# Decoder layer on one core: folded keys copied out of the banks by ScalarE alone, with the order of calls laid anew

## The chip, the cores and the metric

The kernel runs on one core of a Trainium2 chip. A core has five engines that each work through their own list of instructions in order and meet only through semaphores: TensorE (PE, matmuls, with its weight loads PEld), VectorE (DVE), ScalarE (ACT), GpSimd (POOL) and SyncE (SP), which here only issues DMAs. The metric is the device time of one execution in microseconds, lower is better. Before the change it is 623.12 us, the median of three runs (623.07 to 624.21).

## The reference

One decoder layer on 8 elements of 256 tokens with 256 channels, all fp32:

```python
x = x + attn(layernorm(x), W_q, W_k, W_v, W_o)      # 16 heads of 16, rotary, causal
x = x + xattn(layernorm(x), ctx, ctx, mask,         # 16 heads of 64 over 77 context rows
              W_Q, W_K, W_V, W_O)
x = x + ffn(layernorm(x))                           # 256 -> 1024 -> 256, exact gelu

# in ffn both linears are
Wq = fake_quant_weight(W)                           # 8 bits, one scale for the tensor
base = jnp.einsum('bsi,oi->bso', x, Wq) + b
lora = jnp.einsum('bsr,or->bso', jnp.einsum('bsi,ri->bsr', x, A), B)
return base + SCALING * lora
```

The part that the change touches is the cross-attention's keys. `softmax((x W_Q)(ctx W_K)^T / 8)` is computed as `x (W_Q (ctx W_K)^T)`: the query weight is folded into the keys once, at the start, for all elements. The folded keys are a matrix of 256 rows and 16 heads x 616 context rows.

## The kernel before, in words

Every fp32 product is made of three matmuls, because each operand is held as a hi piece and a lo piece: hi x hi, hi x lo, lo x hi (`product`, L732 to L734). So a result of TensorE that is used again is first copied out of its bank as the hi piece by ScalarE (`copy`, L1409), and then VectorE or GpSimd takes the difference as the lo piece (`low`, L1846; GpSimd L548, L555, L569).

The work is software-pipelined over the 8 elements. Each engine runs `first()`, then five times `step(a, b, n, m)`, then `drain()`; in a step element a is in its causal attention, b in its cross-attention and feed-forward, n in its projections, m in its first norm. Each engine's `first`, `step` and `drain` is a list of calls written out by hand; nothing else sets the order. Between engines only the semaphore waits in the called functions hold.

`first()` covers 0 to about 218.6 us: loads and splits of all weights, the folded keys, the values of the context (`values2`), the projections of elements 0 to 3, the causal attention of 0 to 2, and cross-attention and feed-forward of element 0. The calls that matter here:

- `keys(m)`, m = 0 to 7: TensorE makes the keys of two heads (12 matmuls of 128x308); ScalarE copies the hi piece `kT` out (0.68 us), VectorE the lo piece.
- `fold(m, k)`, k = 0, 1: TensorE multiplies them with the query weight (L777, `wo_hi`/`wo_lo` in the trace, since that memory holds the query weight first), in two halves. The bank pairs 3/4 and 5/6 are used in turn, so a half waits until the half two places before is copied out. The copy goes to one of three places in SBUF (`fold_slots`: two in `ck_raw`, one in `work`), from which SP's `store_folded` sends it to DRAM (L351); a place is free again when its store has landed (`fold_st`).
- Of the 32 halves, ScalarE copies the 16 with k = 0 and VectorE the 16 with k = 1 (L1819).
- `scores(a, g, ..)` (L883) makes scores in three banks by turns, and VectorE's `maxima(a, h)` (L1893, two per g) finds the row maxima; `scores` of g waits for the maxima two heads before. After `transpose_max`, ScalarE's `maxima(a)` and SP's `shifts(a)`, `shifted(a, g)` (L904) makes the scores again, less their maxima, and ScalarE takes the exponential (`exponentials`, L1442). For elements 0 to 2 `shifted` has one pair of banks, so each waits for the exponential before it.
- `rotary` (VectorE, L1877), `rotate` (GpSimd, L563, L564, L569) and `rotated` (ScalarE) make the rotated q and k; SP stores them (`store_rotated`) and loads them back in stacked form (`stacks`).
- `statistics_b`, `inverse_deviation` (GpSimd, L574) and `norm_b` (VectorE, L1841) make the norm ahead of the cross-attention (`norm_b(b, 0)`) and the feed-forward (`norm_b(b, 1)`).
- `quantise` (VectorE, L1760 to L1766) rounds `wpj_raw` and `wfc_raw`, three passes each; GpSimd's `split_lo` (L548) makes the lo pieces of the context, WV, WO, WO2 and the projection weight.

Of the kernel before, what the change touches and what calls it, by code (L numbers as in the profile page):

```python
# [38 lines left out]
def decoder_layer(nc, x, ctxT, mask, wqT, wkT, wvT, woT, wQT, wK, wV, wO, wfcT, bfc, Afc, BfcT,  # L39
# [25 lines left out]
    with ExitStack() as ctx:  # L65
# [251 lines left out]
        def _(sp):  # L317
# [116 lines left out]
            def first():  # L434
                first_input()
                weight(QKV_W)
                weight(CTX_W)
                weight(WK_W)
                lora_columns()
                trig_tables()  # L440
                load_x(1)
                weight(WQ_W)
                weight(PJ_W)
                store_rotated(0)
                weight(WV_W)
                load_x(2)
                stacks(0, 0)
                residual_input(0)
                store_folded(0, 0)
                weight(WO_W)  # L450
                store_folded(0, 1)
                stacks(0, 1)
                store_folded(1, 0)
                store_folded(1, 1)
                store_folded(2, 0)
                store_folded(2, 1)
                store_rotated(1)
                store_folded(3, 0)
                shifts(0)
                store_folded(3, 1)  # L460
                store_folded(4, 0)
                store_folded(4, 1)
                store_folded(5, 0)
                load_x(3)
                store_folded(5, 1)
                store_folded(6, 0)
                stacks(1, 0)
                store_folded(6, 1)
                store_folded(7, 0)
                store_folded(7, 1)  # L470
                stacks(1, 1)
                weight(WO2_W)
# [3 lines left out]
                weight(FC_W)  # L476
                biases()
                context_values(0)
                store_rotated(2)
                stacks(2, 0)  # L480
                load_x(4)
                stacks(2, 1)
                context(1)
                residual_input(2)
                store_rotated(3)
                shifts(2)
                stacks(3, 0)
                stacks(3, 1)
                context_values(1)
# [25 lines left out]
        def _(pool):  # L515
# [90 lines left out]
            def first():  # L606
                inverse_deviation(rs_a, lna_ve, lna_rs, 0)
                split_lo(CTX_W)
                rotate(0, 0)
                inverse_deviation(rs_a, lna_ve, lna_rs, 1)  # L610
                rotate(0, 1)
                rotate(1, 0)
                rotate(1, 1)
                lora_rows()
                inverse_deviation(rs_a, lna_ve, lna_rs, 2)
# [4 lines left out]
                split_lo(WV_W)  # L620
                causal(0, 4)
                causal(0, 5)
                causal(0, 6)
                causal(0, 7)
                split_lo(WO_W)
# [103 lines left out]
        def _(pe):  # L729
# [1597 lines left out]
```

## Time and profile before

| | us |
|---|---|
| median of 3 runs | 623.12 |
| the profiled execution | 619.42 |
| its span (first to last instruction) | 617.7 |
| TensorE busy | 498.4 (81%) |
| VectorE busy | 389.0 (63%) |
| ScalarE busy | 291.4 (47%) |
| GpSimd busy | 252.5 (41%) |
| granted TensorE clock, mean | 0.953 of full speed |

TensorE has the largest share of busy time and 60% of the chain that ended last. The shares are means over stages of very different make. In the first 218.6 us the kernel prepares everything that is shared by all elements, and TensorE stands still more often; from there the five steps follow each other at about 63 us (the last two are shorter, 60 us), and then the drain of 88.8 us. A wait counts where it stands on TensorE in a stage in which nothing else is ahead of it; idle time of the other engines costs nothing by itself. A granted clock under 1 in a stage means that for part of it TensorE ran at 1.2 instead of 2.4 GHz.

### The profile page before, as it was taken

The page shows a single profiled execution, that of the slowest core. Times are in us where ns is not written, and L with a number is a line of the kernel's source. Part 1 is how long each engine was busy: PE and PEld are TensorE (multiplying, and loading weights), DVE is VectorE, ACT ScalarE, POOL GpSimd, SP SyncE. Part 2 cuts the span into 40 slices and gives each one's busy share as a digit, 9 for nine tenths or more (in the row PEclk, how much of TensorE's full clock was granted, in tenths as well). Part 3 has the DMA queues.
Part 4 walks back from the last instruction along what each step waited for, and adds up shares of the span by engine and source line. Part 5 has one row for each costly group of instructions (what it writes and reads, how often), then busy time and mean ns, then how long its engine had stood idle before and what let it go on. Part 6 is the DMA issues. An engine that isn't in the chain of part 4 may idle for free.

```text
span 617.7 us, 11686 instructions
## 1 busy us (share of the span) xinstructions
PE 498.4 (81%) x4320; PEld 416.9 (67%) x4320; DVE 389.0 (63%) x1079; ACT 291.4 (47%) x464; POOL 252.5 (41%) x351
## 2 busy tenths in 40 slices
PE   3577889599857879798879887988797879688986
PEld 3566667366646667587758865886586758677876
DVE  5669533877785089448945795479536943767532
ACT  4324454335455425482548344833583448343724
POOL 5551162537163633346234632464245134525310
PEclk9798999889977999899989998999999989899999
DMA  8696479355220414061406140714070210300000
GB/s 299 203 259 253 184 238 267 119 198 133 59 85 4 109 67 136 25 120 52 135 14 131 52 136 2 142 51 118 5 140 19 83 40 2 101 2 21 1 19 17
DMA packets 57496, 62.40 MB, mean 101 GB/s; under 512 B 6832, under 2 KB 52544, under 8 KB 57440
## 3 DMA queue, kind: packets, MB, share of 16 engines
q1 hardware_dynamic: 55936, 56.71, 33.1%
q0 software_dynamic: 1504, 4.95, 2.2%
q8 instruction: 34, 0.56, 0.4%
q14 instruction: 22, 0.18, 0.1%
HBM read 38.28 MB, written 23.10 MB: 99 GB/s over the span
## 4 chain that ended last, share of the span: by engine, by line
PE 60%; DVE 19%; ACT 6%; issue 6%; POOL 2%; DVEq 0%; POOLq 0%; ACTq 0%
PE banks L732 11%; PE banks L733 10%; PE banks L734 10%; PE banks L996 6%; PE banks L1054 5%; DVE banks L1893 3%; PE banks L1007 3%; PE banks L883 2%; DVE c_lo L1846 2%; PE banks L979 2%; PE banks L904 2%; ACT probs L1442 2%; DVE work L1841 1%; DVE mx L1956 1%; DVE work L1962 1%
## 5 line engine op out<-in xcount | busy, mean ns | idle before, releaser
L1893 DVE CUSTOM_DVE_ANT_0 banks<-banks,causal_qk 128x256 f32<-128x256 f32 (+1 forms) x256 | 83.7, 388 | 12.1 <-PE banks L883 7.6
L589 POOL TENSOR_SCALAR_AFFINE_SELECT probs<-probs 128x256 f32<-128x256 f32 x128 | 49.5, 414 | 100.0 <-ACT probs L1442 99.6
L578 POOL TENSOR_TENSOR work<-work,rc 128x616 f32<-128x616 f32 x32 | 39.9, 1247 | 105.0 <-DVE rc L1970 105.0
L1442 ACT ACTIVATE probs<-banks 128x768 f32<-128x768 f32 x64 | 50.8, 811 | 31.3 <-PE banks L904 27.4
L1409 ACT ACTIVATE work<-banks 128x1024 f32<-128x1024 f32 (+1 forms) x34 | 32.6, 962 | 34.2 <-PE banks L996 33.9
L555 POOL TENSOR_TENSOR ck_lo<-ck_raw,ck_hi 128x308 fp32r<-128x308 f32 x56 | 47.9, 881 | 0.0
L1846 DVE TENSOR_TENSOR c_lo<-banks,c_hi 128x512 fp32r<-128x512 f32 x32 | 22.0, 688 | 40.1 <-ACT c_hi L1409 40.1
L883 PE MATMUL banks<-k_stack,q_stack 62*128 62x256 f32 (+1 forms) x256 | 28.9, 304 | 22.2 <-DVE mneg L1893 22.2
L996 PE MATMUL banks<-ident,work 128*128 128x128 f32 (+1 forms) x256 | 36.9, 291 | 10.3 <-DVE c_lo L1846 9.5
L732 PE MATMUL banks<-wo_hi,c_hi 128*128 128x256 f32 x128 | 39.8, 311 | 6.1 <-DVE c_lo L1846 5.6
L1409 ACT ACTIVATE c_hi<-banks 128x512 fp32r<-128x512 f32 x32 | 19.2, 599 | 52.3 <-PE banks L1007 44.2
L883 PEld LDWEIGHTS banks<-k_stack,q_stack 62*128 62x128 f32 x256 | 20.0, 191 | 34.7 <-DVE mneg L1893 21.1
L1474 ACT ACTIVATE work<-work 128x616 f32<-128x616 f32 x32 | 22.9, 716 | 41.1 <-DVE work L1962 41.1
L996 PEld LDWEIGHTS banks<-ident,work 128*128 128x128 f32 (+1 forms) x256 | 30.1, 150 | 15.4 <-issue 13.7
L904 PE MATMUL banks<-q_stack,k_stack 64*128 64x128 f32 (+1 forms) x256 | 30.4, 322 | 9.9 <-ACT probs L1442 8.9
L732 PE MATMUL banks<-ck_hi,xbT_hi 128*128 128x308 f32 x112 | 37.9, 339 | 0.0
L732 PE MATMUL banks<-wpj_hi,hid_hi 128*128 128x256 f32 x128 | 37.9, 296 | 0.0
L733 PE MATMUL banks<-wo_lo,c_hi 128*128 128x256 f32 x128 | 37.1, 290 | 0.0
L734 PE MATMUL banks<-wo_hi,c_lo 128*128 128x256 f32 x128 | 36.8, 288 | 0.0
L733 PE MATMUL banks<-wpj_lo,hid_hi 128*128 128x256 f32 x128 | 36.5, 285 | 0.0
L734 PE MATMUL banks<-wpj_hi,hid_lo 128*128 128x256 f32 x128 | 36.4, 285 | 0.0
L1893 DVE DVE_READ_ACCUMULATOR2_ANT mneg<- 128x1 f32 x256 | 36.1, 141 | 0.0
(223 smaller groups left out, 1595.0 us busy)
## 6 DMA issues: line engine op xcount, KB each, us to landing
ck_raw<-ck_dram SPq DMA_DIRECT2D x28, 308.0 KB, 4.5
ck_dram<-ck_raw SPq DMA_DIRECT2D x11, 616.0 KB, 3.5
rot_dram<-rot_s_hi SPq DMA_DIRECT2D x16, 256.0 KB, 2.1
rot_dram<-rot_s_lo SPq DMA_DIRECT2D x16, 256.0 KB, 2.1
q_stack<-rot_dram SPq DMA_DIRECT2D x32, 128.0 KB, 3.5
k_stack<-rot_dram SPq DMA_DIRECT2D x32, 128.0 KB, 3.3
ck_dram<-work SPq DMA_DIRECT2D x5, 616.0 KB, 4.1
v<-v_dram SPq DMA_DIRECT2D x8, 308.0 KB
```

What stands on the lines that cost most here:

```text
L555: last = pool.tensor_tensor(ck_low(b, k, g), raw, ck_high(b, k, g).bitcast(F32), ALU.subtract)
L578: pool.tensor_tensor(sc2[g % 2], sc2[g % 2], rc2[:, g % 2].rearrange("p q a -> p q a ()").broadcast_to([P, QT, 4, S2]), ALU.mult).then_inc ...
L589: last = pool.affine_select(out=diagonal, in_=diagonal, compare_op=ALU.is_ge, fill=0.0, base=0, pattern=[[0, 2], [1, P]], channel_multipli ...
L732: pe.matmul(dst, w[0], x_[0], start=first, stop=False, **kw)
L733: pe.matmul(dst, w[0], x_[1], start=False, stop=False, **kw)
L734: return pe.matmul(dst, w[1], x_[0], start=False, stop=last, **kw)
L883: mm = pe.matmul(halves(banks[p])[:, 1 - q, 0:keys_q], q_stack[rows, g, q * P:(q + 1) * P], k_stack[rows, g, 0:keys_q], start=(q == 1), st ...
L904: mm = pe.matmul(halves(bk + p)[:, 1 - k, k * P:T], k_stack[rows, g, k * P:(k + 1) * P], q_stack[rows, g, k * P:T], start=(k == 1), stop=( ...
L996: mm = pe.transpose(bank[0:width, 5 + c, p * T + q * P:p * T + (q + 1) * P], sc2[g % 2].rearrange("p q a s -> p (q a s)")[:, at:at + width ...
L1409: act.activation(dst, src, ACT.Copy).then_inc(done, 1)
L1442: act.activation(probs[:, n:n + 2, :], bank[:, bk:bk + 2, P:4 * P], ACT.Exp, scale=SCALE).then_inc(p_ok, 1)
L1893: last = dve.tensor_tensor_reduce(out=scores_q, in0=scores_q, in1=causal_qk[:, 1 - q:2].rearrange("p a n -> p (a n)"), scale=-1.0, scalar= ...
```

## The change

VectorE's `fold` is removed, and ScalarE's `fold` gets k as a parameter and copies all 32 halves. The same banks, places and semaphores are used; VectorE keeps `keys`, the lo pieces. Beside this the lists of calls in `first()` are written in another order on all five engines, and two calls change places in `step()`.

```diff
-            def fold(m, half):
-                i = KD * m
-                act.wait_ge(fold_ps, 4 * m + half + 1)
+            def fold(m, k, half):
+                i = KD * m + k
+                act.wait_ge(fold_ps, 2 * i + half + 1)
                 if half == 0 and i >= FS:
                     act.wait_ge(fold_st[i % FS], 16 * (i // FS))
-                at = 3 + 2 * ((5 * m + 1 + half) % 2)
-                copy(folded(i, half), bank[:, at:at + 2, 0:HS].rearrange("p a (b s) -> p b a s", s=S2), fold_ok[0])
+                at = 3 + 2 * ((5 * m + 3 * k + 1 + half) % 2)
+                copy(folded(i, half), bank[:, at:at + 2, 0:HS].rearrange("p a (b s) -> p b a s", s=S2), fold_ok[k])
...
-            def fold(m, half):                       # VectorE
-                i = KD * m + 1
-                dve.wait_ge(fold_ps, 4 * m + half + 3)
...
-                dve.tensor_copy(folded(i, half), bank[:, at:at + 2, 0:HS].rearrange("p a (b s) -> p b a s", s=S2)) \
-                    .then_inc(fold_ok[1], 1)
```

On SP the loads at the start, and on TensorE the calls up to the first scores, read:

```diff
 first_input()                      # SP
+weight(WK_W)
+weight(CTX_W)
+load_x(1)
 weight(QKV_W)
-weight(CTX_W)
-weight(WK_W)
-lora_columns()
 trig_tables()
-load_x(1)
 weight(WQ_W)
...
 project(0, 0)                      # TensorE
+keys(0)
 project(0, 1)
-project_v(0)
-keys(0)
 fold(0, 0)
 keys(1)
+fold(0, 1)
+fold(1, 0)
+project_v(0)
+keys(2)
 transpose_a(1)
-fold(0, 1)
+fold(1, 1)
 project(1, 0)
+fold(2, 0)
+keys(3)
 project(1, 1)
-fold(1, 0)
-keys(2)
 scores(0, 0, 2)
```

Further on, TensorE's `lora_down(0)` and `lora_down(1)` move from between the shifted scores of element 0 to behind `transpose_a(2)` and `scores(1,0)`; `output_a(0)` and `project(2,0)` move ahead of `values2(1)`, and `values2(2)` behind `scores(1,0)`; and the four `hidden(0, g)`, which stood behind `scores(2,4)`, `scores(2,7)` and `transpose_max(2)`, stand behind `scores(2,2)`, `scores(2,3)`, `scores(2,5)` and `transpose_max(2)`. On SP `context(1)` moves ahead of `store_rotated(2)`. In `step()` ScalarE's `hidden(b,3)` goes ahead of `context_keys(b+1,3)` and VectorE's `context_lo(b,0)` ahead of `maxima(a,6)`.

ScalarE's list from the keys of m = 5 to the last exponentials of element 0, before (`ck_raw` and `work` are the fold copies, `kT` the keys, `probs` the exponentials):

```order
L1409 ACTIVATE kT<-banks 128x616
L1442 ACTIVATE probs<-banks 128x768
L1409 ACTIVATE ck_raw<-banks 128x616 x2
L1409 ACTIVATE kT<-banks 128x616
L1442 ACTIVATE probs<-banks 128x768 x2
L1409 ACTIVATE ck_raw<-banks 128x616
L1442 ACTIVATE probs<-banks 128x768
L1409 ACTIVATE ck_raw<-banks 128x616
L1442 ACTIVATE probs<-banks 128x768 x2
L1409 ACTIVATE kT<-banks 128x616
```

and now, from the keys of m = 6:

```order
L1409 ACTIVATE kT<-banks 128x616
L1380 ACTIVATE wo_hi<-wo_raw 128x512
L1409 ACTIVATE work<-banks 128x616
L1442 ACTIVATE probs<-banks 128x768
L1409 ACTIVATE work<-banks 128x616
L1442 ACTIVATE probs<-banks 128x768
L1409 ACTIVATE ck_raw<-banks 128x616
L1442 ACTIVATE probs<-banks 128x768 x2
L1409 ACTIVATE ck_raw<-banks 128x616
L1409 ACTIVATE kT<-banks 128x616
L1442 ACTIVATE probs<-banks 128x768 x2
L1409 ACTIVATE rot<-banks 128x512
```

The first exponential stood behind the keys of m = 5 and stands behind those of m = 6 and the first half of the last fold of m = 5, with the copies of both k among the exponentials.

GpSimd's list from the rotation of element 2 (`rot`) over the stores of the context's values (`v_dram`) to the keys of element 0, before:

```order
L569 TENSOR_TENSOR rot_s_lo<-rot,rot_s_hi 128x512
L544 DMA v_dram<-work 128x1024 x4
L544 DMA v_dram<-v 104x1024
L574 TENSOR_TENSOR rs_b<-rs_b,half_a 128x2
L555 TENSOR_TENSOR ck_lo<-ck_raw,ck_hi 128x308 x2
```

and now:

```order
L569 TENSOR_TENSOR rot_s_lo<-rot,rot_s_hi 128x512
L544 DMA v_dram<-work 128x1024 x3
L548 TENSOR_TENSOR wo_lo<-wo_raw,wo_hi 128x2048
L544 DMA v_dram<-work 128x1024
L574 TENSOR_TENSOR rs_b<-rs_b,half_a 128x2
L544 DMA v_dram<-v 104x1024
L555 TENSOR_TENSOR ck_lo<-ck_raw,ck_hi 128x308 x2
```

The lo split of the output weight WO2 (`wo_lo` 128x2048) now stands between these stores; it stood behind the last `affine_select` of element 1.

GpSimd's list around the second deviation of element 0 (`rs_b`, from `statistics_b(0,1)`), before:

```order
L574 TENSOR_TENSOR rs_b<-rs_b,half_a 128x2
L563 TENSOR_TENSOR rot<-probs 128x256
L564 TENSOR_TENSOR rot<-probs 128x256
L569 TENSOR_TENSOR rot_s_lo<-rot,rot_s_hi 128x512
L548 TENSOR_TENSOR wpj_lo<-wpj_raw,wpj_hi 128x2048
L574 TENSOR_TENSOR rs_a<-rs_a,half_a 128x2
```

and now:

```order
L574 TENSOR_TENSOR rs_b<-rs_b,half_a 128x2
L548 TENSOR_TENSOR wpj_lo<-wpj_raw,wpj_hi 128x2048
L574 TENSOR_TENSOR rs_a<-rs_a,half_a 128x2
L563 TENSOR_TENSOR rot<-probs 128x256
L564 TENSOR_TENSOR rot<-probs 128x256
L569 TENSOR_TENSOR rot_s_lo<-rot,rot_s_hi 128x512
```

The lo split of the feed-forward's second weight moved from behind the rotation of element 3 to right behind that deviation.

## Rows read from the trace of the kernel before

**Rows 1.** Busy time by stage: start:end, length, five engines with counts, PEclk, DMA share, GB/s.

```profile
0.00:24.80 24.80, 8.99 (x52) 8.13 (x53) 16.67 (x25) 10.63 (x10) 16.64 (x23) 0.97 0.74 249
24.80:89.80 65.00, 52.08 (x444) 42.22 (x444) 38.45 (x109) 26.60 (x39) 22.74 (x33) 0.90 0.74 236
89.80:128.30 38.50, 29.13 (x169) 22.93 (x168) 24.81 (x99) 14.06 (x26) 14.28 (x19) 0.88 0.62 180
128.30:150.80 22.50, 21.50 (x215) 16.27 (x215) 17.23 (x25) 12.32 (x17) 12.66 (x21) 0.98 0.62 183
150.80:169.80 19.00, 15.94 (x142) 13.55 (x140) 15.43 (x20) 6.22 (x11) 6.70 (x5) 1.00 0.33 86
169.80:194.00 24.20, 15.97 (x103) 13.68 (x100) 19.59 (x89) 12.74 (x23) 10.86 (x9) 0.79 0.17 56
218.60:528.90 310.30, 263.84 (x2428) 221.25 (x2427) 204.24 (x620) 158.13 (x259) 128.35 (x190) 0.98 0.29 72
```

**Rows 2.** Groups of instructions, 24 to 92 us: count, busy us, mean ns, idle before.

```profile
L1409 ACT ACTIVATE ck_raw<-banks 128x616 f32<-128x616 f32 x10 | 6.8, 684 | 12.2 <-PE banks L777 12.2
L1442 ACT ACTIVATE probs<-banks 128x768 f32<-128x768 f32 x8 | 6.5, 812 | 4.1 <-PE banks L904 4.0
...
L1819 DVE COPY ck_raw<-banks 128x616 f32<-128x616 f32 x12 | 9.3, 792 | 3.0 <-PE banks L777 3.0
...
L1846 DVE TENSOR_TENSOR kT<-banks,kT 128x616 fp32r<-128x616 f32 x8 | 6.4, 798 | 16.7 <-ACT kT L1409 16.7
```

**Rows 3.** TensorE's waits, 24.8 to 89.8 us: total us, times, longest.

```profile
PE banks L777 <- DVE kT L1846: 6.9, 4, 4.4
PE banks L883 <- DVE mneg L1893: 4.5, 3, 2.4
PE banks L777 <- ACT ck_raw L1409: 1.9, 2, 1.2
PE banks L732 <- ACT work L1409: 1.5, 2, 1.3
PE banks L904 <- ACT probs L1442: 0.9, 1, 0.9
PE banks L777 <- DVE ck_raw L1819: 0.8, 2, 0.7
PE banks L777 <- DVE work L1819: 0.4, 1, 0.4
```

**Rows 4.** Timeline, ScalarE then TensorE: start, length, instruction, idle before and releaser.

```profile
11.36 1.91 ACT L1380 ACTIVATE hid_hi<-hid_raw 128x2048 fp32r<-128x2048 f32 x1 [0.82 <-DMA hid_raw<-in_wK]
...
24.81 0.88 PE L777 MATMUL banks<-kT,wo_hi 64*128 64x308 f32 x4 [4.36 <-DVE kT L1846]
...
31.52 0.56 PE L777 MATMUL banks<-kT,wo_hi 64*128 64x308 f32 x4 [0.75 <-ACT ck_raw L1409]
```

**Rows 5.** TensorE, 89.8 to 128.3 us: a wait, then `values2(3)` and what follows.

```profile
PE banks L883 <- DVE mneg L1893: 5.1, 5, 1.1
...
107.74 0.50 PE L732 MATMUL banks<-wfc_hi,ck_hi 128*128 128x512 f32 x1
...
110.73 0.45 PE L883 MATMUL banks<-k_stack,q_stack 62*128 62x256 f32 x4
```

**Rows 6.** Line 1760's durations (ns, min/median/max, first and last start); GpSimd's timeline.

```profile
L1760 DVE TENSOR_SCALAR wpj_raw<-wpj_raw,winv x1: 1285/1285/1285, 57.4 to 57.4; 128x2048 f32<-128x2048 f32 x1
L1760 DVE TENSOR_SCALAR wfc_raw<-wfc_raw,winv x1: 4975/4975/4975, 148.8 to 148.8; 128x2048 f32<-128x2048 f32 x1
...
148.14 4.58 POOL L548 TENSOR_TENSOR wo_lo<-wo_raw,wo_hi 128x2048 fp32r<-128x2048 f32 x1
```

**Rows 7.** 169.8 to 194 us: TensorE's longest wait; `norm_b(0,1)` and GpSimd beside it.

```profile
PE banks L883 <- DVE mneg L1893: 5.8, 5, 2.5
...
176.54 1.46 DVE L1841 TENSOR_SCALAR work<-x,mv_b,rs_b 128x256 f32<-128x256 f32 x2 [0.16 <-POOL rs_b L574]
...
177.08 0.77 POOL L564 TENSOR_TENSOR rot<-probs 128x256 f32<-128x256 f32 x1
```

More of the change, by code:

```diff
@@ L1160, in first @@
                 shifted(1, 0)
-                lora_down(3)
                 shifted(1, 1)
@@ L1528, in first @@
[L1528 to L1545 removed]
+                fold(0, 1, 0)
@@ new lines, in first @@
+                fold(0, 1, 1)
+                fold(1, 0, 0)
+                fold(1, 0, 1)
+                split_hi(WV_W)
+                keys(2)
+                xaT_part(1)
+                values(0)
+                fold(1, 1, 0)
+                fold(1, 1, 1)
+                fold(2, 0, 0)
+                keys(3)
+                fold(2, 0, 1)
+                rotated(1, 0)
+                fold(2, 1, 0)
+                fold(2, 1, 1)
+                fold(3, 0, 0)
+                fold(3, 0, 1)
@@ L1546, in first @@
+                keys(4)
+                fold(3, 1, 0)
+                fold(3, 1, 1)
+                fold(4, 0, 0)
+                fold(4, 0, 1)
+                maxima(0)
+                keys(5)
+                rotated(1, 1)
+                fold(4, 1, 0)
+                fold(4, 1, 1)
+                fold(5, 0, 0)
+                fold(5, 0, 1)
+                keys(6)
+                split_hi(WO_W)
+                fold(5, 1, 0)
                 exponentials(0, 0, 2)
-                fold(5, 0)
@@ L1991, in first @@
             def first():
+                clear_queries()
                 statistics_a(0)
-                clear_queries()
                 norm_a(0)
+                split_lo(WK_W)
+                xaT_part(0)
                 split_lo(QKV_W)
-                xaT_part(0)
+                statistics_a(1)
                 rotary(0, 0)
-                statistics_a(1)
-                split_lo(WK_W)
-                rotary(0, 1)
-                norm_a(1)
                 split_lo(WQ_W)
                 keys(0)
+                rotary(0, 1)
+                keys(1)
+                norm_a(1)
                 largest(1, PJ_W)
-                keys(1)
+                keys(2)
                 xaT_part(1)
-                fold(0, 0)
                 rotary(1, 0)
-                fold(0, 1)
+                statistics_a(2)
+                keys(3)
                 rotary(1, 1)
-                keys(2)
+                largest_of_all(1)
+                norm_a(2)
                 maxima(0, 0)
@@ L2084, in first @@
                 norm_b(0, 0)
+                clear_values()
+                norm_a(3)
                 xbT_part(0, 0)
-                clear_values()
                 add_lora(1, PJ_W, 2)
                 softmax2(0, 0)
+                softmax2(0, 1)
+                sums2(0, 0)
                 add_lora(1, PJ_W, 3)
-                sums2(0, 0)
-                softmax2(0, 1)
-                norm_a(3)
+                statistics_a(4)
                 largest(0, FC_W)
```

350 lines of the change are left out of this document (158 added, 192 removed).

## The prediction

> **What bounds the kernel now.** I read the stages first, then TensorE's waits inside them, then the instructions behind the waits. In the table of stages [rows 1] the reader is to see TensorE's busy time against each stage's length: 263.84 of 310.30 us in the five periodic steps, but 9.0 of 24.8, 52.1 of 65.0, 29.1 of 38.5, 15.9 of 19.0 and 16.0 of 24.2 us in parts of the start-up (0 to 218.6 us), at a granted clock of 0.90, 0.88 and 0.79 in three of them. No other engine is full there: in the fold stage VectorE has 38.5 of 65 us, ScalarE 26.6. TensorE works through an in-order list and waits for hand-overs. The steps keep their order but for two calls: `context_keys(b+1,3)` goes behind `hidden(b,3)`, and `context_lo(b,0)` ahead of one `maxima`. TensorE's waits in a step stand at other places (scores on `mneg`, `c_lo` of later groups), so I cost both at nothing; if that cover fails, 0.3 us a step, 1.5 in all, either way. What can be won or lost lies in the start-up, where TensorE is idle for about 55 us in all.
>
> **The copies themselves.** VectorE loses 16 copies of 0.79 us, 12.7 us in all; ScalarE gains 16 of 0.68, 10.9 us [rows 2]. Its load in the fold stage goes from 26.6 to 37.5 of 65 us. TensorE's waits for VectorE's copies were 0.8 + 0.4 = 1.2 us [rows 3], so the move alone is worth 1.2 at most; VectorE's free time counts only where VectorE was late with something else. That a copy on ScalarE ends 0.1 us sooner is worth nothing: the ring of two bank pairs hides it behind the next fold's matmuls, and would give 16 x 0.1 without them.
>
> **Term 1, up to the first fold (24.8 us before).** TensorE's last wait here was 4.36 us, for `kT` [rows 4]. Now the keys' weight and the context are loaded first, and the 0.79 MB of q, k and v weights stand behind x[1], which waits for the first norm (about 6.8 us). The bytes up to and with them are 3.0 MB; before, 2.7 MB had landed when ScalarE could split `hid_raw` at 11.36 us [rows 4]. So they land near 11.9; their hi and lo splits cost 1.5 and 1.8 us in the timeline, and `project(0,0)` starts at 15.2 instead of 10.4. It takes 2.6 us (twelve matmuls at 1.2 GHz, as before), `keys(0)` 1.75 and `project(0,1)` 1.4: 21.0. The lo pieces of the folded query weight and of the keys are ready about 22.3. The first fold so starts 2.5 us before its old 24.81, but `project_v(0)` (1.4 to 1.7) is still owed: +1.0. Bounds: the weights land 2 us later, -1.0; everything 1 us sooner with the earlier norm, +2.0.
>
> **Term 2, the fold stage, 24.8 to 89.8.** Item by item, walking TensorE's new list by hand with the old durations:
> - VectorE's copies are no longer waited for: +1.2 [rows 3].
> - `kT` (hi on ScalarE, then lo on VectorE, 0.68 + 0.80 [rows 2]) left 2.5 us of waits after the first one (6.9 less 4.36), in three places. Now only `keys(1)` and `keys(6)` have nothing but a first half of a fold between them and the half that needs their bank: 1.7. +0.8.
> - The first fold and `keys(1)` ran at 1.2 GHz after the 4.36 us gap: four matmuls in 0.88 us that take 0.56 later [rows 4]. Both together took 5.2 us where 3.1 do. The gap is now about 1.3 us: +2.1.
> - `scores(0,0)` stands right behind `project(1,1)` and waits until `rotary(1,1)` has read it, two VectorE instructions of 0.69: -1.4.
> - Score waits were 4.5 [rows 3]. Now `largest_of_all` and `norm_a(2)` stand on VectorE ahead of the first `maxima`, and two passes of the quantisation (1.3 and 1.2 us) among the others; I find waits of 1.9, 1.0, 1.7, 0.5 and 0.4, together 5.5. -1.0.
> - Waits for ScalarE were 1.9 + 1.5 + 0.9 = 4.3 [rows 3]. The eight exponentials of 0.81 [rows 2] have fewer of TensorE's folds between them than before (two and one `keys`, where five and two `keys` stood), so I find five waits of 0.4 to 1.1 (3.2 in all) and 0.8 where two folds now follow each other. +0.3.
> Sum +2.0. Bounds: of 12.9 us idle at most 5 can go, as the chains above stay; at worst ScalarE, serving folds and exponentials in one line, adds five waits of its 0.68, and the sum is -1.4.
>
> **Term 3, 89.8 to 128.3.** `values2(2)` (107.74 to 110.73 for its like, 3.0 us [rows 5]) no longer stands ahead of `scores(1,0)`, one `lora_down` (1.0) does: 2.0 sooner. VectorE sets this stage: TensorE waits 5.1 us for its maxima. VectorE takes in two `add_lora` and `up_weights` and gives `statistics_a(3)` away, +0.9 us of work. +1.0. What hides the rest: the v stores on GpSimd's queue slip behind a split of 4.58 us, which still ends before `clear_values` wants them; without that cover, -1. SP's `lora_columns` moves behind `shifts(0)`, 20 us ahead of its reader. Bounds -1 to +2. The stage after it has TensorE busy 21.5 of 22.5 us [rows 1]: nothing.
>
> **Term 4, the quantisation of `wfc`.** Its first step took 4.975 us, the same form on `wpj_raw` 1.285 [rows 6]. GpSimd's `wo_lo` split ran from 148.14 to 152.72; VectorE's instruction ends 1.1 us after it, near its own undisturbed length: it stood still meanwhile. Behind it stand `attention(1)` and `c_lo`, for which TensorE then waited. The split moves some 40 us ahead, beside maxima. VectorE wins up to 3.7 us; TensorE's idle time in the stage is 3.06 [rows 1], and some 0.5 of that stays for the c pieces: +2.5, bounds 0 and 3.0. SP now holds `context(1)` ahead of `store_rotated(2)`, to about 144 us instead of 130; its reader is at 165 or later, so that is hidden.
>
> **Term 5, scores of element 2, 169.8 to 194.** The four `hidden` now go between the scores. By VectorE's pace (0.72 a `maxima`) and some 2 us a `hidden` this fills waits (5.8 us [rows 7]); 2.1 us for `residual_a(1)` and `rotary(3,1)` now stand ahead of the first score. Together +0.7. But the split of `wpj` (4.57 us) moves ahead of `rotate(3,1)` on GpSimd, right behind the deviation that `norm_b(0,1)` needs, and VectorE does 2.1 us of other work before that norm. The norm pair took 1.46 us instead of 0.8 where it met GpSimd's `rot`, ending 0.1 us after it [rows 7]. Here it would end 4 us late, of which 2.8 reach TensorE: 0.7 - 2.8 = -2.1. Bounds -4 and +3.
>
> The Trainium skill (SBUF — State Buffer, section "SBUF: two separate sides") has VectorE and GpSimd share one pair of ports under a lock, not by shares: who starts first keeps it for the whole instruction. By that rule term 5 is -2.1; if both only slowed each other it would be near -0.5. The 4.975 us row agrees with the lock.
>
> **Sum.** 1.0 + 2.0 + 1.0 + 2.5 - 2.1 = 4.4 us. The profiled execution took 619.42 (span 617.7 and 1.7 around it), so 615.0 by its own measure. It lies 3.7 under the median of 623.12 of the runs shown, and I take the difference to the median: 618.7.
>
> **Rivals.**
> *A, ScalarE becomes what TensorE waits for (slower).* Place: 60 to 90 us, where exponentials (0.81) and fold copies (0.68) share one in-order engine, and a `shifted` waits for the exponential before it, which may stand behind a copy. For: ScalarE's share rises to 58% of the stage, and TensorE has less between. Against: one wait of 0.9 us for exponentials is all there was. The point from which it decides: term 2 holds, and 4.4 is gone, when seven of the sixteen moved copies show a whole wait of 0.68 each; with ten, 4.4 - 6.8 = -2.4: 625.5.
> *B, the gain is hidden.* The start-up ends by the chain through stored keys: `context(0)` waits until every folded key has landed, and the DMA engines are 0.74 busy in the stage [rows 1]. For: nothing in front of them is sped up. Against: the keys were loaded by 103 us and first used at 114.7, 11 us of slack. Terms 2 and 3 then vanish: 4.4 - 3.0 = 1.4, and within the same spread term 5 a little worse, 0.5: 622.6.
> *C, the denser order also keeps the clock.* The stages at 0.90, 0.88 and 0.79 [rows 1] had short matmuls between waits; at 0.97 their busy 52, 29 and 16 us shrink by 7, 9 and 18%, 3.6 + 2.6 + 2.9 = 9, of which 2.1 is in term 2. With half of the rest, 3.5: 615.2. For: 1.2 GHz followed the gap before the first fold. Against: waits of 1 us remain in all three.
> *D, norm and split don't meet,* as `norm_b(0,1)` comes first: term 5 is +0.7, so 615.9.
>
> **How the numbers follow.** Forecast 0.42, A 0.17, B 0.14, C 0.15, D 0.12. Time 618.7. The forecast's own range is 616.5 to 621.5; the whole range 614.0 to 624.0 takes in B, D, C's middle and A up to its break-even, and leaves out A's worse and C's better part. 0.2% (1.25 us) is about what a measurement of this kernel can tell from no change. Faster 0.70 (C, D, the forecast, and a little of B), same 0.13 (most of B and a rest), slower 0.17 (A).
>
> **What would show it.** In the profile after: the first fold at 21.5 to 23; `turn_a(0)` near 84 instead of 89.8 with the last fold behind it; the first quantisation step of `wfc_raw` under 2 us; `norm_b(0,1)` stretched to 3 us or more beside the `wpj` split; `project(4,0)`, the start of the first step at 218.6, near 214.3, and all behind it shifted as a block, with steps of 63 us. I am wrong if the steps change in length, if waits for ScalarE between 24 and 90 us exceed 8 us (A), or if the first step starts early and the end does not.

## The result

The changed kernel takes 631.1 us by the median of its first runs (630.0 to 640.4) against 623.1 for the kernel before: ratio 1.0129, interval 1.0082 to 1.0177. Two later measurements on other chips gave 1.016 (1.0106 to 1.0214) and 1.0165 (1.0128 to 1.0201). The forecast was 618.7, faster. It was wrong in sign: about 12 us lie between.

The profile shown here is that of a later execution of the changed kernel, 629.86 us with a span of 628.0 at a mean granted clock of 0.947, because the first profiled one (640.4 us, clock 0.922) was in the slower state that some executions of these kernels fall into; the ratios leave such executions out, the medians count them. First its table of stages, which answers to [rows 1]: start to first fold, to `turn_a(0)`, to `scores2(0,0)`, to `turn_a(1)`, to the end of the context output, to the last `maxima`, to the first step, and the five steps. The first step is cut at `transpose_b(1,0)` from here on, in every kernel; in before that is 220.1 us, 1.5 behind the 218.6 of [rows 1].

```profile
0.00:24.00 24.00, 8.29 (x40) 7.74 (x40) 15.55 (x20) 8.88 (x7) 12.33 (x19) 1.00 0.77 267
24.00:91.10 67.10, 49.97 (x437) 40.58 (x437) 33.55 (x101) 36.83 (x56) 27.80 (x37) 0.90 0.72 224
91.10:133.70 42.60, 31.97 (x187) 24.95 (x188) 29.35 (x97) 14.61 (x26) 17.46 (x18) 0.93 0.59 166
133.70:157.90 24.20, 21.29 (x190) 16.13 (x190) 14.16 (x26) 12.51 (x18) 12.87 (x23) 0.91 0.31 97
157.90:178.00 20.10, 18.91 (x176) 16.25 (x176) 14.29 (x25) 9.82 (x15) 4.62 (x5) 1.00 0.73 173
178.00:204.00 26.00, 15.50 (x87) 13.37 (x88) 21.27 (x83) 9.07 (x18) 14.21 (x14) 0.71 0.15 48
204.00:231.70 27.70, 22.63 (x194) 18.16 (x193) 6.59 (x13) 12.68 (x20) 9.93 (x22) 0.84 0.26 67
231.70:540.90 309.20, 262.25 (x2417) 220.00 (x2416) 202.57 (x618) 157.85 (x259) 128.63 (x190) 0.98 0.30 73
```

The copies moved as forecast: in the fold stage VectorE fell from 38.5 to 33.6 us busy, ScalarE rose from 26.6 to 36.8. The steps took 309.2 us against 308.8 for before, with TensorE idle 46.9 and 46.5 us of it: the two calls that change places in `step()` cost nothing, as forecast. The loss is in the start-up: the first step begins at 231.7 instead of 220.1. Two rows of TensorE alone split it:

```profile
0.00:220.10 220.10, 164.10 (x1307) 0.91 0.56 171
```

for the kernel before (length, TensorE busy with its count, granted clock, DMA share, GB/s), and for the changed one

```profile
0.00:231.70 231.70, 168.55 (x1307) 0.90 0.54 162
```

The same 1307 instructions are recorded. TensorE is idle 63.1 us instead of 56.0, and busy 168.6 instead of 164.1. So 7.1 of the 11.6 us are waits, and 4.5 are the same matmuls, run longer at a lower granted clock. The two parts don't lie in the same place. Up to `scores2(0,0)` TensorE is busy 90.2 us in both kernels (663 instructions each), and what is lost there is 5.4 us of waits. Behind it, from 133.7 us, it is busy 78.3 us in place of 73.9, at a granted clock of 0.86 in place of 0.92:

```profile
133.70:231.70 98.00, 78.33 (x645) 0.86 0.34 91
```

This split into idle and busy time is used all through. Idle time of one kernel came within 0.6 us for the changed kernel (63.1 and 63.7) and for l1 (60.8 and 61.1), and 3.0 us apart for e3 and m4, for a reason shown below; busy time came 3.7 to 5.3 us apart.

TensorE's waits in the fold stage, against [rows 3]:

```profile
PE banks L777 <- DVE kT L1853: 5.5, 6, 1.7
PE banks L883 <- DVE mneg L1900: 4.6, 3, 2.6
PE banks L904 <- ACT probs L1442: 2.0, 2, 1.1
PE banks L883 <- DVE probs L1884: 1.5, 1, 1.5
PE banks L732 <- ACT ck_raw L1409: 1.1, 3, 0.4
PE banks L917 <- POOL probs L589: 1.0, 1, 1.0
PE banks L929 <- ACT rot L1409: 0.7, 1, 0.7
PE banks L777 <- ACT ck_raw L1409: 0.7, 2, 0.4
```

VectorE's copies (`ck_raw`, L1819 before) are gone from the list; `kT`, `rotary`'s `probs`, GpSimd's `probs` and `rot` are new or longer.

Now the two places where VectorE meets a long GpSimd split, in the timeline (start, length, instruction, idle before and what ended it). A split is GpSimd's `split_lo`, about 4.6 us long for 2048 columns. The first is the `WO2` split beside `mask_bias(0)`, line 1938, which copies the uint8 mask into bf16:

```profile
112.00 5.32 DVE L1938 TENSOR_SCALAR mask_bf<-mask_u 128x308 bf16<-128x308 uint8 x2
...
112.31 4.60 POOL L548 TENSOR_TENSOR wo_lo<-wo_raw,wo_hi 128x2048 fp32r<-128x2048 f32 x1
...
118.66 0.44 PE L883 MATMUL banks<-k_stack,q_stack 62*128 62x256 f32 x4 [3.02 <-DVE mneg L1900]
```

These two copies are 0.31 us each elsewhere:

```profile
L1938 DVE TENSOR_SCALAR mask_bf<-mask_u x16: 308/312/5092, 112.0 to 565.3; 128x308 bf16<-128x308 uint8 x16
```

`maxima` stand behind them in VectorE's list, and `scores(1,2)` waits 3.02 us for one. The second place answers to [rows 7], the `wpj` split beside `norm_b(0,1)`:

```profile
179.00 4.50 POOL L548 TENSOR_TENSOR wpj_lo<-wpj_raw,wpj_hi 128x2048 fp32r<-128x2048 f32 x1
...
179.96 4.01 DVE L1848 TENSOR_SCALAR work<-x,mv_b,rs_b 128x256 f32<-128x256 f32 x2
...
180.14 0.45 PE L883 MATMUL banks<-k_stack,q_stack 62*128 62x256 f32 x4 [2.81 <-DVE probs L1884]
...
184.03 0.47 PE L961 MATMUL banks<-ident,work 128*128 128x128 f32 x1 [3.44 <-DVE work L1848]
```

The norm pair takes 4.01 us and ends 0.5 us behind the split, where it took 1.46. And the quantisation step of `wfc` that stood still beside a split in [rows 6] (4975 ns) does so no longer:

```profile
L1776 DVE TENSOR_SCALAR wfc_raw<-wfc_raw,winv x1: 1235/1235/1235, 156.5 to 156.5; 128x2048 f32<-128x2048 f32 x1
```

### The profile page after: what moved, and what is told of

It is laid out like the page before. It is cut to its first block, busy times and chain, and to the rows that moved or that the text cites. A ratio compares the mean times of both kernels' runs of the same rounds, so it can differ in the third digit from the quotient of the medians.

```text
span 638.4 us, 11686 instructions
## 1 busy us (share of the span) xinstructions
PE 511.5 (80%) x4320; PEld 427.5 (67%) x4320; DVE 383.8 (60%) x1063; ACT 301.7 (47%) x480; POOL 252.8 (40%) x351
## 4 chain that ended last, share of the span: by engine, by line
PE 50%; DVE 12%; ACT 3%; issue 3%; POOL 2%; DVEq 0%; POOLq 0%
PE banks L732 9%; PE banks L733 8%; PE banks L734 8%; PE banks L1054 6%; PE banks L996 5%; PE banks L1007 3%; PE banks L883 2%; DVE c_lo L1853 2%; PE banks L979 2%; DVE work L1848 1%; DVE banks L1900 1%; DVE work L1969 1%; DVE mx L1963 1%; PE banks L1062 1%; PE banks L904 1%
## 5 line engine op out<-in xcount | busy, mean ns | idle before, releaser
L1409 ACT ACTIVATE work<-banks 128x1024 f32<-128x1024 f32 (+1 forms) x38 | 35.3, 933 | 43.0 <-PE banks L996 34.5
L883 PE MATMUL banks<-k_stack,q_stack 62*128 62x256 f32 (+1 forms) x256 | 31.4, 327 | 24.5 <-DVE mneg L1900 20.2
L883 PEld LDWEIGHTS banks<-k_stack,q_stack 62*128 62x128 f32 x256 | 21.6, 208 | 37.9 <-DVE mneg L1900 22.4
L569 POOL TENSOR_TENSOR rot_s_lo<-rot,rot_s_hi 128x512 fp32r<-128x512 f32 x16 | 20.5, 1278 | 54.3 <-ACT rot_s_hi L1409 54.3
```

The costliest lines, as they stand in the source:

```text
L883: mm = pe.matmul(halves(banks[p])[:, 1 - q, 0:keys_q], q_stack[rows, g, q * P:(q + 1) * P], k_stack[rows, g, 0:keys_q], start=(q == 1), st ...
L1409: act.activation(dst, src, ACT.Copy).then_inc(done, 1)
```

## The experiments

"Early" is each engine's list up to the last fold and `turn_a(0)`, "late" is what stands behind it up to the first step. Idle and busy are TensorE's, from the start to `transpose_b(1,0)` in the profiled execution of each kernel, worked out from the table of stages as above. The time is the median of all runs of a kernel, the ratio is to the kernel before on the same chip, with its interval. Kernels measured on one chip are c_after (the changed kernel), e1, e2, e3; h1, h2, l1, b1; c2 (the changed kernel again), l1b, l2, l3; and m1 to m4. e3 and m4 are one kernel, and so are l1 and l1b.

| kernel | early / late order | time | ratio | idle | busy |
|---|---|---|---|---|---|
| before | old / old | 621.2 to 622.4 | 1 | 56.0 | 164.1 |
| changed (two measurements) | new / new | 633.2, 632.4 | 1.016, 1.0165 | 63.7, 63.1 | 172.3, 168.6 |
| e1 | old / old, ScalarE copies | 622.5 | 0.996 (0.992 to 1.000) | 56.5 | 163.8 |
| e2 | new / new, VectorE copies | 625.3 | 1.003 (1.001 to 1.006) | 63.9 | 167.9 |
| e3, m4 | old / old, WO2 split early | 617.8, 616.6 | 0.994, 0.990 | 57.2, 54.2 | 168.9, 164.5 |
| b1 | e1 and e3 together | 618.5 | 0.993 (0.990 to 0.997) | 53.8 | 167.0 |
| h1 | new / old | 623.2 | 1.002 (0.999 to 1.005) | 60.3 | 165.3 |
| h2 | old / new | 625.0 | 1.003 (0.998 to 1.008) | 59.5 | 172.6 |
| l1, l1b | new / new, both calls moved | 619.1, 620.8 | 0.996, 0.999 | 60.8, 61.1 | 168.2, 162.9 |
| l2 | new / new, mask moved | 624.3 | 1.002 (0.999 to 1.005) | 61.3 | 165.2 |
| l3 | new / new, wpj split moved | 629.0 | 1.011 (1.006 to 1.016) | 63.6 | 167.9 |
| m1 | old / new, both moved | 621.2 | 0.998 (0.994 to 1.002) | 56.6 | 166.9 |
| m2 | new / old, WO2 split early | 622.9 | 1.001 (0.997 to 1.004) | 58.3 | 163.9 |
| m3 | l1 and rotary(3,1) earlier | 624.6 | 1.000 (0.996 to 1.005) | 61.4 | 172.9 |

**Copies or order.** Four kernels on one chip. The changed kernel once more:

> The changed kernel again, to see it in an undisturbed profile beside the others. Theory O (the new order costs the time: a late first projection, pauses between short matmuls that keep TensorE at 1.2 GHz in 40 to 140 us, two waits ahead of the scores of element 2): 1.010 to 1.016 of before, mean granted clock near 0.945 against 0.953, the first step about 10 us later than before's 218.6. Theory S (ScalarE as the one server of copies costs it): the same total, but TensorE's waits for ScalarE between 24 and 95 us would be above 8 us instead of about 4.

633.2 us: the loss is real. Its first step begins at 236.0, as late as a lower clock in the start-up makes it (idle 63.7 us).

The order of before with all copies on ScalarE:

```diff
-def fold(m, half):          # ScalarE, k = 0 of each pair; VectorE had k = 1
+def fold(m, k, half):       # ScalarE, both; behind the same keys(...) calls
```

> The order of calls of before on all engines, with ScalarE making all 32 fold copies (its 16 new copies stand where TensorE's folds stand). Theory S: this alone shows the loss, 1.008 to 1.016 of before. Theory O: the move of the copies is worth at most the 1.2 us that TensorE waited for VectorE's copies and costs at most five waits of 0.68 us: 0.998 to 1.005.

622.5 against 622.1 for before by the medians, ratio 0.996 (0.992 to 1.000). In the old order ScalarE as the server costs nothing; the copies' move gives nothing sure either. Its waits in the fold stage tell why:

```profile
PE banks L777 <- DVE kT L1853: 8.0, 4, 4.4
```

The 1.2 us of waits for VectorE's copies are gone, and `kT` has 1.1 us more than its 6.9 in [rows 3]. All of it stands at one place, `keys(4)`, where the wait is 1.98 us in place of 0.81. It is not ScalarE's new queue: ScalarE had been idle for 2.12 us when it made the hi piece. The lo piece waited on VectorE, behind a pass of the quantisation:

```profile
58.59 0.68 ACT L1409 ACTIVATE kT<-banks 128x616 fp32r<-128x616 f32 x1 [2.12 <-PE banks L734]
...
59.08 1.23 DVE L1778 TENSOR_SCALAR wpj_raw<-wpj_raw 128x2048 f32<-128x2048 f32 x1
60.21 0.80 DVE L1853 TENSOR_TENSOR kT<-banks,kT 128x616 fp32r<-128x616 f32 x1
...
61.16 0.55 PE L777 MATMUL banks<-kT,wo_hi 64*128 64x308 f32 x4 [1.98 <-DVE kT L1853]
```

TensorE came to this place 2.0 us earlier, by saved waits and faster matmuls, and VectorE's pass, which kept its place in the list, took part of that back.

The changed order with VectorE making its copies again:

```diff
+fold(0, 0)                  # VectorE, behind keys(1), and so on to fold(7, 1)
-fold(0, 1, 0)               # ScalarE, and the other fifteen of k = 1
```

> The new order on all engines, with VectorE making the 16 copies of k = 1 again (each stands where TensorE's fold stands in the list). Theory O: the loss stays or grows, since the order leaves VectorE's work where it was without copies: 1.010 to 1.020 of before. Theory S: the loss goes, 0.998 to 1.004.

625.3 us, ratio 1.003 (1.001 to 1.006), and idle time 63.9, the same as with ScalarE's copies (63.1, 63.7). The two measures speak for different theories. By idle time the extra waits of 7 us come from the order alone. By total time the result lies in the range of theory S (0.998 to 1.004) and not in that of theory O (1.010 to 1.020): about 8 us of the loss are gone with the copies back on VectorE. In the profiles that gain is not where the copies are. The start-up is as long as the changed kernel's (231.8 and 231.7 us), and the span is 4.4 us shorter because the five steps, with the same calls in them, took 304.7 us in place of 309.2. Why e2 has the faster executions is not shown. Its runs fall in two heaps: seven at 623.7 to 625.7 (granted clock 0.955 to 0.960) and three at 634.7 to 636.6 (0.937 to 0.940). The changed kernel had no run above 0.947 in twelve.

The order of before with the WO2 split alone moved, twice (the second time in the last set):

```diff
 store_values(2)
+split_lo(WO2_W)             # GpSimd
 ...
 causal(1, 7)
-split_lo(WO2_W)
```

> Before, with one call moved: GpSimd's lo split of WO2 (4.58 us) stands between the stores of the context's values, as in the changed kernel, not beside the quantisation of wfc. Term 4 of the prediction by itself: the first quantisation pass falls from 4.97 us to under 2, TensorE's waits between 150.8 and 169.8 us from 3.1 to about 1, and the time by 2.5 us: 0.996 (0.995 to 0.999). If attention and c_lo were late for another reason: 1.000.

> The kernel before with the WO2 split alone moved behind store_values(2), once more, as the measure for the others: 617 to 619, ratio to before 0.99 to 0.997.

617.8 and 616.6 us, ratios 0.9938 (0.9904 to 0.9973) and 0.9896 (0.9833 to 0.9960): the best version of the study. From `scores2(0,0)` to the first step, in before and in m4:

```profile
128.30:220.10 91.80, 73.91 (x645) 0.92 0.35 101
```

```profile
129.90:218.70 88.80, 73.68 (x644) 0.90 0.38 107
```

17.9 us of idle time become 15.1. The profiled execution of m4 is 5.4 us shorter than that of before, but only 1.4 of it lies in the start-up; the steps took 304.9 us in place of 308.8, which the moved call does not touch. So 2.8 us are shown as fewer waits; the rest of the 4 to 6 us is not waits, and not shown to come from the moved call.

In e3's profile the idle time there was 19.3, with a wait of 3.4 us for `up_x`. It is the same kernel as m4. In e3 the small instruction ahead of `up_x` on VectorE began 0.37 us behind the `wpj` split on GpSimd:

```profile
180.30 4.54 POOL L548 TENSOR_TENSOR wpj_lo<-wpj_raw,wpj_hi 128x2048 fp32r<-128x2048 f32 x1
...
180.67 4.20 DVE L1834 TENSOR_SCALAR rs_b<-mv_b 128x2 f32<-128x2 f32 x1
```

and in m4 at the same moment as the split:

```profile
180.61 0.17 DVE L1834 TENSOR_SCALAR rs_b<-mv_b 128x2 f32<-128x2 f32 x1
...
180.62 4.58 POOL L548 TENSOR_TENSOR wpj_lo<-wpj_raw,wpj_hi 128x2048 fp32r<-128x2048 f32 x1
```

In e3 the instruction of two columns ended with the split, after 4.20 us; 0.4 us earlier, in m4, the same one took 0.17.

**Where in the order.** New early order and old late order:

```diff
 # each engine: the changed kernel's calls to fold(7, 1) / causal(0, 7) / attention(0),
 # then the calls that are left, in the order of before
```

> All 32 folded copies by ScalarE; each engine's list up to the last fold in the changed kernel's order, and all calls behind it (from project_v(1) and attention_lo(0) to the first step) in the order of before. Theory 1 (the loss is spread: the changed trace was 4.4 us late at turn_a(0) and 15.9 at the first step): turn_a(0) near 94, first step (transpose_b(1,0)) near 224 instead of 236, time 626. Theory 2 (the loss is made early, and the later stages only pass on a bad phase of TensorE's clock): turn_a(0) at 94 and still over 630. Theory 3 (the early order alone is harmless, as it was forecast): at most 623.

> All 32 folded copies by ScalarE; each engine's list up to turn_a(0) in the order of before, and all calls behind it in the changed kernel's order (both early splits on GpSimd with it). Theory 1: turn_a(0) at 89.8 as before, the mask's copy on VectorE and norm_b(0,1) stretched beside the two splits, first step near 231, time 630 or more. Theory 2: under 625. Theory 3 (the WO2 split's gain of 4 us outweighs the rest): 618 to 621.

The mirror image is h2. The first steps came at 225.6 and 232.1 us, near theory 1 (224 and 231), and the times of 623.2 and 625.0 under its forecasts (626, and 630 or more). h2 has two heaps, five executions at 620.4 to 621.4 and five at 628.6 to 630.6, so its median says little. Idle time adds within 0.4 us: over e1 (56.5) the new early order has 3.8 us more, the new late order 3.0, sum 6.8; both together measure 6.6 and 7.2. Time may not: 0.55% and 0.67% over e1's ratio make 1.2%, both together cost 2.0%. The intervals of the ratios, 0.3 to 0.5% each way, make this gap of 0.8% no larger than its own error, so it is not shown; if it is there, it is not waits.

Both calls that meet a split moved out of its way:

```diff
 # VectorE
-mask_bias(0)                # behind maxima(1, 2)
+mask_bias(0)                # behind maxima(1, 13)
 # GpSimd
-split_lo(PJ_W)              # ahead of rotate(3, 1)
+split_lo(PJ_W)              # behind rotate(3, 1)
```

> The changed kernel with two calls moved: the mask's copy on VectorE goes behind maxima(1,13), out of the way of the WO2 split on GpSimd, and the split of wpj goes back behind rotate(3,1) on GpSimd. Lock theory: the mask's copy is 0.31 us instead of 5.1, the 3.0 us wait for mneg falls to 1.0; norm_b(0,1) under 1.5 us, TensorE's wait of 3.4 for it under 1; together 4.5 us less than the changed kernel, about 628.5. Rival (VectorE had the time, TensorE is paced by something else): less than 1.5 us.

619.1 us, where the changed kernel had measured 633.2 on another chip: 14 us, and I had expected 4.5. The wait for `norm_b(0,1)` fell to 0.56 us, but the split met the next thing:

```profile
181.30 0.66 PE L961 MATMUL banks<-ident,work 128*128 128x128 f32 x4 [0.56 <-DVE work L1848]
```

```profile
193.64 0.43 DVE L1900 CUSTOM_DVE_ANT_0 banks<-banks,causal_qk 128x256 f32<-128x256 f32 x1 [0.40 <-PE banks L883]
...
196.48 1.49 DVE L1909 CAST mneg_s<-mneg 128x32 fp32r<-128x32 f32 x1
198.00 0.77 DVE L1853 TENSOR_TENSOR mneg_s<-mneg,mneg_s 128x32 fp32r<-128x32 f32 x1
```

The split ran from 193.43 to 197.93. The `maxima` beside it kept their 0.43 us; the small cast took 1.49 (0.23 in the changed kernel), and TensorE's wait for `mneg_s` grew from 2.1 to 3.9. Since the chips differed, four kernels shared one next:

> The changed kernel once more, on the chip of the three below, since the run without the two stretched instructions (619.1) and the changed kernel (633.2) had not shared a chip. If the gap is real: 628 to 635, its runs at a granted clock of 0.938 to 0.947. If it was the chip's: within 2 us of the kernel without them.

> The kernel with both calls moved once more, beside the changed kernel. If the gap is real: 617 to 625, its runs at a granted clock of 0.95 to 0.968, idle time of TensorE up to the first step 60.8 us against 63.7. By idle time alone it should win 2.9 us; what it wins beyond that is the clock. If it was the chip's: within 3 us of the changed kernel.

> The changed kernel with the mask's copy alone moved behind maxima(1,13). Theory W (waits add up, the clock is noise): TensorE's 3.0 us wait at scores(1,2) goes, idle time before scores2(0,0) 8.1 instead of 10.4, gain 2.3 us. Theory K (the wait also sets off a slow stretch of the clock): gain 5 to 12 us, near 622 to 628.

> The changed kernel with the split of wpj alone back behind rotate(3,1). norm_b(0,1) 1.1 us instead of 4.0 and TensorE's wait 0.6 instead of 3.4, but split_max(2) then stands beside the split, and the wait for it is 3.9 instead of 2.1: 1 us by waits (theory W), 630 to 633. My forecast had charged 2.8 to it. Theory K: 5 us or more, if the 3.4 us wait is what sets the clock down there.

632.4, 620.8, 624.3 and 629.0 us. The gap is real, and the two calls add by the medians: 8.1 for the mask, 3.4 for the split, 11.6 for both, each good to 3 or 4 us by the intervals, so that the split's 3.4 is not clear of noise. By idle time the mask is worth 1.8 to 2.5 us (before `scores2(0,0)` 10.6 falls to 8.1) and the split nothing (19.7 and 19.8 from `scores2(0,0)` on): that wait only moved. So most of both is busy time, the clock. For the mask the time is what theory K gave (5 to 12 us), for the split it lies between W (1) and K (5 or more). That the wait sets the clock down, which K says, is not shown. A part of the busy time can be placed. The same stretch, from the last `maxima` of element 2 to `turn_a(2)`, in the changed kernel and in l3:

```profile
200.40:224.30 23.90, 19.86 (x157) 0.74 0.31 79
```

```profile
201.40:224.10 22.70, 17.80 (x156) 0.84 0.24 58
```

In the five traces with the split ahead of `rotate(3,1)` on GpSimd and ScalarE's copies (three of the changed kernel, h2, l2) this stretch has 19.7 to 19.9 us busy; in four with it behind (l1, l1b, l3, m1) 17.7 to 17.8. Two fall out: m3 (22.6, behind) and e2 (17.0, ahead). So 2.0 us go with the split's place in all but these two, as work at the lower level of the clock right behind it (granted 0.74 and 0.84 in the two rows). They are not the gain of l3's profile, though: its start-up is 0.2 us shorter than the changed kernel's in all (231.5 and 231.7), as other stretches were longer, and 4.2 us lie in the steps (305.0 and 309.2). For the mask I found no such stretch: the next stage comes at 19.5 us (granted 1.00) or at 20.9 to 21.3 (0.91 to 0.93), with and without the stretched copy.

The steps show the clock by itself: 46.9 to 47.3 us idle in the traces of nearly all kernels, and 257.8 to 262.3 busy. The five steps of l1b:

```profile
224.00:530.60 306.60, 259.39 (x2415) 0.99 0.30 73
```

They are 2.6 us shorter than the changed kernel's 309.20, with the same calls in the same order. From one `transpose_b` to the next the first part of a step takes 40.2 to 40.5 us or 41.4 to 42.1, in any kernel, and the second part repeats to 0.1 us (21.4 in the first three steps). How many of the five first parts are short makes the difference between 304.7 and 309.2.

**Whether the parts add.** The old early order with the new late one, both calls moved:

```diff
 # h2 with mask_bias(0) and split_lo(PJ_W) as in l1
```

> ScalarE makes all copies; up to turn_a(0) the order of before, behind it the changed kernel's, with the mask's copy behind maxima(1,13) and the wpj split behind rotate(3,1). If the early order costs what TensorE's idle time says (17.1 us in the fold stage against 12.9): idle time up to the first step 57, 4 us less than the 61.1 of the version with the new early order, time 616 to 617. If the early order costs nothing by itself: 620.5. If its cost sits in the clock's luck: anywhere from 615 to 625, with an idle time of 57.

```profile
0.00:223.50 223.50, 166.91 (x1306) 0.89 0.56 168
```

Idle 56.6, as forecast to half a microsecond, and 621.2 us, no faster than l1 and l1b. This fits the third case: the new early order costs 4.5 us of waits, and here busy time took the gain back (166.9 against 162.9 in l1b). By the time alone the second case (620.5) fits as well.

```diff
 # h1 with split_lo(WO2_W) behind store_values(2)
```

> The changed kernel's order up to the last fold, the order of before behind it, with the WO2 split right behind store_values(2). The same hybrid with the split late measured 623.2 with 60.3 us of idle time. If the split's move is worth the same here as alone in before (about 4 us, idle time 2.8 less): 619, idle time 57.5. If it then meets the mask's copy on VectorE: the copy is stretched to 5 us, and 622 or more.

Idle 2.0 less than h1 and the mask's copy at 0.31, but 622.9 against 623.2 us (on another chip; ratios 1.0005 and 1.0017). The move that gave 4 to 6 us in before gives nothing sure here.

```diff
 rotary(3, 0)                # VectorE
+rotary(3, 1)
 residual_b(0)
 statistics_b(0, 1)
 residual_a(1)
-rotary(3, 1)
```

> The version without the two stretched instructions (620.75), with rotary(3,1) on VectorE right behind rotary(3,0), ahead of residual_b(0), statistics_b(0,1) and residual_a(1). If the 2.8 us wait of scores(2,0) costs its length: idle time 58.3 instead of 61.1, time about 618. If VectorE is the bound there, the two residuals only come later and delay norm_b(0,1) and the first maxima: idle time 60 or more, 620 to 621.

```profile
180.23 0.44 PE L883 MATMUL banks<-k_stack,q_stack 62*128 62x256 f32 x4 [3.01 <-DVE x L1932]
```

The wait is as long and now for `residual_a(1)`: VectorE is the bound there, and 624.6 us is no gain. The last, ScalarE's copies and the WO2 split in the order of before:

> The order of before, with all 32 folded copies by ScalarE and the WO2 split on GpSimd right behind store_values(2), nothing else moved. If both single edits add (-0.4% and -0.6% measured one by one): near 616, and faster than either. If what the copies' move gave was only the clock's luck: near 618, as the WO2 move alone. If the two disturb each other as the whole change did: 622 or more.

618.5 us and idle 53.8, the least of all, yet no faster than the WO2 move alone.

## Why the prediction was wrong

The forecast sum was a start-up 4.4 us shorter; it came 11.6 longer. Three of its steps failed. Term 2 priced the chain behind `keys` at its two instructions and found it in the way at two places, 1.7 us; it stood in the way at five, 5.2 us. Term 3 moved a split "beside maxima" and overlooked `mask_bias(0)` among them, which took 5.09 us instead of 0.31. And the clock was counted only as a gain, where it cost 4.5 us. By terms, in idle time:

| term | forecast gain | measured | by |
|---|---|---|---|
| 1, to the first fold | 1.0 | 0.1 | idle 15.8, then 15.7 |
| 2, fold stage, waits | -0.1 | -4.2 | 12.9, then 17.1 |
| 3, to `scores2(0,0)` | 1.0 | -1.2 | 9.4, then 10.6; 8.1 without the mask's stall (l2) |
| to `turn_a(1)`, costed at nothing | 0 | -1.9 | 1.0, then 2.9 |
| 4, to the context output | 2.5 | 2.6 | 3.1, then 0.5; 0.9 in m4 |
| 5, to `turn_a(2)` | -2.1 | -2.5 | 12.7, then 15.2 |
| clock, start-up | 2.1 (in term 2) | -4.5 | busy 164.1, then 168.6 |

*Term 1.* The weights had landed when ScalarE split them at 13.13 us, not at 11.9, and `project(0,0)` started at 16.6, not 15.2:

```profile
13.13 1.48 ACT L1380 ACTIVATE wqkv_hi<-wqkv_raw 128x1536 fp32r<-128x1536 f32 x1 [2.39 <-DMA wqkv_raw<-in_wvT]
```

I had taken landing as bytes at the rate of before. The first fold so came at 24.0 us, not at 22.3. This size was off within its bounds.

*Term 2 is the first step that failed*, and in the item on `kT`. `keys(1)` and `keys(6)`, the two places that I had found, cost 2.8, and `keys(2)`, `keys(4)` and `keys(5)` wait as well, 2.4 together: 5.2 in place of 1.7, where before had 2.5. It is the order and not ScalarE's longer queue: e2, with VectorE's copies back, has the same waits.

```profile
PE banks L777 <- DVE kT L1846: 5.7, 6, 1.7
```

I had priced the chain at its two instructions, 1.48 us, and let any call between `keys` and the half fold cover it; a `transpose_max` or a `transpose_a` is shorter than that. And the chain is longer than its two instructions where the order puts something ahead of one of them. At `keys(1)` and `keys(5)` the hi piece stood on ScalarE behind a copy of `rotated` and behind `maxima(0)` (0.7 and 0.9 us late), at `keys(4)` the lo piece on VectorE behind `maxima` (1.1 us late). The item for the copies is unsure: here the waits for VectorE's copies are gone, but in the old order their 1.2 us came back at `kT` (e1). Rotary's wait came as forecast (1.5 for 1.4), score waits better (4.6 for 5.5), those for ScalarE nearly so (3.8 for 4.0). Not foreseen: 1.0 us for GpSimd's `causal` and 0.7 ahead of `turn_a(0)`. `turn_a(0)` came at 91.1, not 84.

*Term 3.* That the moved split goes "beside maxima" was true and not enough: `mask_bias(0)` stands among them, and the change had itself moved it there, from behind `maxima(1,4)` to behind `maxima(1,2)`. Where the split alone is early (m2, m4) the copies keep their 0.31 us. I had the lock rule in hand and applied it to one neighbour of one split. I asked what the split leaves, and not every instruction that it comes to stand beside. By l2 it is the costliest miss: 8.1 us, of which 1.8 to 2.5 are waits that a walk of VectorE's list could have shown. The rest is busy time, by a way that stays open.

*Behind `scores2(0,0)`* I had counted nothing, as TensorE was busy 21.5 of 22.5 us. That was true of the old order. In the new one, `shifted(1,1)` to `(1,3)` stand closer together, and two waits of 0.9 us for ScalarE's exponentials and 0.8 ahead of `turn_a(1)` appear. A full stage can lose by a new order, only not gain.

*Terms 4 and 5* hold in size. The quantisation step took 1.235 us, and the stage gave 2.6. Norm and split met as forecast, ending together, and the 2.1 us ahead of the first score came as 2.8. The score waits fell from 5.8 [rows 7] to 2.0. But l3 shows that the lock was not the price of that place: behind `rotate(3,1)` the stage has the same 15.2 us idle, since `split_max(2)` then stands beside the split.

*The clock* I had only on the credit side (2.1 in the sum, more in rival C). The item itself came: the first four matmuls of the first fold took 0.55 us where they took 0.88. It was used up before `scores2(0,0)`, where busy time is again that of before (90.2 us), and 4.4 us were lost behind it. The clock is a term of both signs and as large as all waits: busy time of the same 1307 instructions came between 162.9 and 172.9 us over these kernels.

The rivals: A fell (3.8 us of waits for ScalarE in the fold stage and 0.7 at `turn_a(0)`, where 8 was the sign for it; e1 at 0.996), though e2's 8 us of total time remain unexplained. B fell: the early order's waits do reach the end of the start-up, by idle time. C had the right quantity with the wrong sign. D did not occur: the norm and the split met. None of them had what came: waits spread over three stages, VectorE stopped beside a split in its new place, and a lower clock on top.

What stays open: why l2 gains 8.1 us with 2 us less idle time, and why the changed kernel has no run at the higher clock while e2, with an idle time 0.8 us from it, has seven runs in ten there. That waits choose the mode is consistent with l2 and l3, but m1 and m2 (less idle time, no gain) and e2 (the same idle time, 8 us gained) speak against a simple rule.

## What to carry over

When a long GpSimd instruction moves, list every VectorE instruction that will run beside its new place, not only those it leaves; `maxima` on the matmul banks passed unharmed, while a cast, norms, the mask's copy and quantisation in SBUF stood still. When a list is laid anew, price a chain between engines with the queue in front of each of its instructions, not by its instructions alone. And split a difference into TensorE's idle time and busy time, stage by stage, before explaining it: here 7 of 12 us were waits that can be walked in the lists, and in the profiles the gains of e2, l3 and m4 lay for the most part in steps that the edit does not touch.

## What was not expected of the hardware

- Two copies of 308 columns from uint8 to bf16 (0.31 us each) took 5.3 us as a pair beside a GpSimd split of 4.60, and a cast of 32 columns 1.49 instead of 0.23. Reductions on the banks beside the same kind of split kept 0.43. The Trainium skill (SBUF — State Buffer, section "SBUF: two separate sides") lets whoever starts first hold the shared ports for a whole instruction, and counts as VectorE's side only instructions in a two-port mode or with two inputs in SBUF. The norm and the cast agree: they began inside a split and ended just behind it. So do e3 and m4, where 0.37 us too late cost 4.0 us. The mask's copy does not quite: it began 0.3 us ahead of the split, should have kept the ports for its 0.3 us, and took 5.09 (the largest of its row; the second copy took 0.31).
- The granted clock is not a property of the kernel's order alone: with the same instructions and 46.9 to 47.3 us idle, the five steps took 304.7 to 309.2 us, and a stretch of 190 matmuls of the start-up 19.5 us at a clock of 1.00 or 20.9 to 21.3 at 0.91 to 0.93.
- Two heaps of times in one kernel (e2: 623.7 to 625.7 and 634.7 to 636.6; h2: 620.4 to 621.4 and 628.6 to 630.6), each with its own granted clock (e2: 0.955 to 0.960 and 0.937 to 0.940; h2: 0.954 to 0.957 and 0.936 to 0.944).
